# Second feed-forward in chunks beside the attention, one batch behind it

## The reference

```
x = x + attn_a(norm(x))                      # conv, pooled attention, gelu
x = x + ffn(norm(x))                         # first feed-forward
x = x + attn_b(norm(x))
x = x + ffn(norm(x))                         # second feed-forward
ffn(x)    = sum over 8 experts of (silu(x @ wg) * (x @ wu)) @ wd
attn_b(x): scores = q @ k / sqrt(8) + alibi_bias   (-inf for later keys)
           softmax(scores) @ v, then @ w_out
```

## Time and profile before

| | us |
|---|---|
| median of three runs (1867.92 to 1869.69) | 1868.59 |
| profiled execution | 1865.06 |
| its span | 1863.3 |
| TensorE busy | 1688.7 (91%) |
| VectorE busy | 1238.6 (66%) |
| ScalarE busy | 1042.8 (56%) |
| GpSimd busy | 228.8 (12%) |

### The profile page before, as it was taken

How to read it: one execution, slowest core, us unless ns; L and a number is a source line. 1 busy time by engine, 2 the same in 40 slices (tenths; PEclk the granted TensorE clock), 3 DMA queues, 4 the chain that set the end, 5 groups by cost and what they waited for, 6 DMA issues and landing times.

```text
span 1863.3 us, 29609 instructions
## 1 busy us (share of the span) xinstructions
PE 1688.7 (91%) x10268; PEld 1150.8 (62%) x10268; DVE 1238.6 (66%) x2140; ACT 1042.8 (56%) x1695; POOL 228.8 (12%) x456
## 2 busy tenths in 40 slices
PE   4589999999999999958888888887899999999998
PEld 2257677767777877723333333332788888888887
DVE  3558566756676677667777777773566666666665
ACT  3435745565465556526666666666455555555554
POOL 4702000200120011111111111112000000000000
PEclk8699999999999999959999999999899999999999
DMA  5100000000000033240202112010000000000000
GB/s 169 38 1 1 1 1 1 0 0 1 0 0 0 1 101 102 79 113 25 58 25 58 42 30 58 24 26 2 0 1 7 6 0 5 6 6 0 7 6 7
DMA packets 60507, 46.83 MB, mean 25 GB/s; under 512 B 7647, under 2 KB 58222, under 8 KB 60398
## 3 DMA queue, kind: packets, MB, share of 16 engines
q1 hardware_dynamic: 60142, 45.30, 8.4%
q10 hardware_dynamic: 256, 0.10, 0.0%
HBM read 28.20 MB, written 17.17 MB: 24 GB/s over the span
## 4 chain that ended last, share of the span: by engine, by line
PE 79%; DVE 8%; ACT 7%; issue 4%; POOL 2%; DMA 0%; ACTq 0%; DVEq 0%; POOLq 0%
PE ps L783 12%; PE ps L784 12%; PE ps L782 12%; PE ps L789 6%; PE ps L790 6%; PE ps L791 6%; PE ps L896 6%; ACT pr L1187 4%; PE ps L641 4%; DVE negp L1482 4%; PE ps L880 3%; PE ps L855 3%; PE ps L710 2%; PE ps L664 2%; PE ps L717 1%
## 5 line engine op out<-in xcount | busy, mean ns | idle before, releaser
L1415 DVE TENSOR_TENSOR hid<-sg,ps 128x512 f32<-128x512 f32 x512 | 350.5, 685 | 388.6 <-PE ps L784 345.6
L1112 ACT ACTIVATE sg<-ps 128x512 f32<-128x512 f32 x512 | 306.1, 598 | 481.3 <-PE ps L784 477.4
L782 PE MATMUL ps<-xn_hi,w_hi 128*128 128x512 f32 x1024 | 426.0, 416 | 2.2 <-DVE xn_lo L1275 1.4
L784 PE MATMUL ps<-xn_hi,w_lo 128*128 128x512 f32 x1024 | 403.1, 394 | 0.0
L783 PE MATMUL ps<-xn_lo,w_hi 128*128 128x512 f32 x1024 | 402.9, 393 | 0.0
L1187 ACT ACTIVATE pr<-ps 128x1024 f32<-128x1024 f32 (+1 forms) x320 | 295.2, 942 | 161.0 <-PE ps L843 110.1
L1432 DVE TENSOR_TENSOR h_lo<-hid,h_hi 128x512 fp32r<-128x512 f32 x512 | 363.6, 710 | 1.4 <-ACT h_hi L1129 1.2
L1129 ACT CAST h_hi<-hid 128x512 fp32r<-128x512 f32 x512 | 313.9, 613 | 1.2 <-DVE hid L1415 0.9
L1482 DVE TENSOR_REDUCE negp<-ps 128x2 f32<-128x1024 f32 (+2 forms) x224 | 248.8, 1144 | 67.2 <-PE ps L843 36.6
L782 PEld LDWEIGHTS ps<-xn_hi,w_hi 128*128 128x128 f32 x1024 | 193.6, 189 | 55.1 <-issue 10.8
L783 PEld LDWEIGHTS ps<-xn_lo,w_hi 128*128 128x128 f32 x1024 | 193.3, 189 | 52.8 <-issue 11.5
(11 more groups left out here) (161 smaller groups left out, 1463.9 us busy)
## 6 DMA issues: line engine op xcount, KB each, us to landing
qs<-qd SPq DMA_DIRECT2D x64, 96.0 KB
ks<-kd SPq DMA_DIRECT2D x64, 96.0 KB
kd<-qkp SPq DMA_DIRECT2D x16, 256.0 KB, 2.9
qd<-qkp SPq DMA_DIRECT2D x8, 384.0 KB, 2.6
x<-in_hidden SPq DMA_DIRECT2D x4, 512.0 KB, 6.5
raw<-in_Wg SPq DMA_DIRECT2D x4, 512.0 KB, 4.5
raw<-in_Wu SPq DMA_DIRECT2D x4, 512.0 KB, 5.4
raw<-in_Wd SPq DMA_DIRECT2D x4, 512.0 KB, 6.7
```

What stands on the lines that cost most here:

```text
L782: pe.matmul(dst, w_hi[m][:, w], xn_hi[:, h, :], start=True, stop=False)
L784: pe.matmul(dst, w_lo[m][:, w], xn_hi[:, h, :], start=False, stop=True).then_inc(f[sig], 1)
L1112: a.activation(sg[:, c % 2, :], bank(c % 2), ACT.Silu).then_inc(f["silu"], 1)
L1415: v.tensor_tensor(hid[:, c % 4, :], sg[:, c % 2, :], bank(2 + c % 2), ALU.mult).then_inc(f["prod"], 1)
```

## The change

Units 0 to 4 stay as they are, but in unit 4 the first tile's norm, transpose and split for the second feed-forward are made. From unit 5 (`MIX`) on, each turn whose number does not leave 4 when divided by 5 carries one chunk of the second feed-forward, 16 a unit, 176 of the 256 in all; tiles go one batch behind the attention. The other 80 follow after unit 15 (`rest_of_ffn`), with the last batch's results and projection between them. In the mixed turns:

- Scores have one pair of banks (0, 1), jobs another (2, 3), which also takes all transposes; down has bank 4, gate 5, weighed values 6, up 7. A score waits for the exponential of the turn before, a job for the reduction of the turn before, gate for the first gated product of the chunk before, up for the second.
- Silu is replaced: ScalarE takes tanh(gate / 2), VectorE makes (tanh + 1) x gate and then x up, which is twice the product; the tile's result is halved in its copy. In the last 80 chunks silu stays, with a factor 2, and two banks each for gate and up.
- The rest `h_lo` is made by GpSimd, in the last 80 chunks by VectorE.
- Down stands two chunks behind gate and up. Each weigh step stands in the turn after its last exponential (`TURNS_TO`).
- `pr` has two buffers from unit 5 on and `vp` 9 columns a head where it had 32. The loops over pairs of tiles are gone: all is written out.

```diff
+MIX = 5
+CHUNKS = TILES * CH
+FFN_TURNS = [k for k in range(NG_S) if k % 5 != 4]
+BESIDE = (UNITS - MIX) * len(FFN_TURNS)
+S_BANK, J_BANK, Y_BANK, O_BANK = 0, 2, 4, 6
+def chunk_at(n, k):
+    if k < 0:
+        n, k = n - 1, k + NG_S
+    return (n - MIX) * len(FFN_TURNS) + FFN_TURNS.index(k) if n >= MIX and k in FFN_TURNS else None
+def values_at(n):
+    return VALUES_AT if n < MIX else TURNS_TO
+def gate_bank(q):
+    return 5 if q < BESIDE or q % 2 == 0 else 0
+def up_bank(q):
+    return 7 if q < BESIDE or q % 2 == 0 else 1
+Y_AT, STATS_AT, NORM_X_AT, XT_AT = (2, 4), 22, 24, 26
...
+def rest_of_chunk(q):
+    pool.wait_ge(FS[1]["hhi"], q + 1)
+    g.tensor_tensor(h_lo[:, q % 2, :], hid[:, q % 4, :], h_hi[:, q % 2, :].bitcast(F32),
+                    ALU.subtract).then_inc(FS[1]["hlo_pool"], 1)
+for n in range(MIX, UNITS):
+    for k, (st, _) in enumerate(TURNS):
+        if st in MASKED and TURNS_TO[st] == k + 1:
+            mask_step(n, st)
+        if chunk_at(n, k - 1) is not None:
+            rest_of_chunk(chunk_at(n, k - 1))
+        if k == 1:
+            split_max(n * 2 + 1)
+        if k == 9 and n % 2 == 0:
+            norm_of_tile((n - MIX + 1) // 2)
+        if k == 14 and n + 1 < UNITS:
+            split_max(n * 2 + 2)
+for t in range(BESIDE // CH + 1, TILES):
+    norm_of_tile(t)
...
+    def gate_up(q):
+        c, h = q % CH, q // CH % 2
+        w = slice(c * P, (c + 1) * P)
+        if c == 0:
+            pe.wait_ge(f["xlo"], q // CH + 1)
+        if q == 0:
+            pe.wait_ge(T["ctx"], MIX * 2 - 1)
+        if 0 < q <= BESIDE:
+            pe.wait_ge(f["half"], q)
+        if q == BESIDE + 1:
+            pe.wait_ge(T["exp"], UNITS * NG_S)
+        if q >= BESIDE + 2:
+            pe.wait_ge(f["prod"], q - 1)
+        for m, sig, dst in ((0, "gate", bank(gate_bank(q))), (1, "up", bank(up_bank(q)))):
+            if m == 1 and 0 < q <= BESIDE:
+                pe.wait_ge(f["prod"], q)
+            pe.matmul(dst, w_hi[m][:, w], xn_hi[:, h, :], start=True, stop=False)
+            pe.matmul(dst, w_hi[m][:, w], xn_lo[:, h, :], start=False, stop=False)
+            pe.matmul(dst, w_lo[m][:, w], xn_hi[:, h, :], start=False, stop=True).then_inc(f[sig], 1)
+    def down(q):
+        c, t = q % CH, q // CH
+        w, dst = slice(c * P, (c + 1) * P), bank(Y_BANK)
+        pe.wait_ge(f["hhi"], q + 1)
+        if q < BESIDE:
+            pe.wait_ge(f["hlo_pool"], q + 1)
+        else:
+            pe.wait_ge(f["hlo"], q - BESIDE + 1)
+        if c == 0 and t:
+            pe.wait_ge(f["y_out"], t)
+        pe.matmul(dst, w_hi[2][:, w], h_hi[:, q % 2, :], start=(c == 0), stop=False)
+        pe.matmul(dst, w_hi[2][:, w], h_lo[:, q % 2, :], start=False, stop=False)
+        pe.matmul(dst, w_lo[2][:, w], h_hi[:, q % 2, :], start=False, stop=(c == CH - 1)
+                  ).then_inc(f["dn"], 1)
+    def chunk(q):
+        gate_up(q)
+        if q >= 2:
+            down(q - 2)
+    def unit_beside_ffn(n):
+        b, g = divmod(n, NG)
+        more = n < UNITS - 1
+        begins = n % 2 and n > MIX
+        for k in range(NG_S):
+            for c in range(2):
+                if k == FIRST_OF_C[c]:
+                    pe.wait_ge(T[f"m_loaded{c}"], n * 32 + 32)
+            scores(n, k)
+            if k == 3:
+                pe.wait_ge(T["ctx"], n * 2)
+            if k == 4 and g == 0:
+                pe.wait_ge(T["c_out"], b * 2 - 1)
+            if k == 4 and begins:
+                pe.wait_ge(f["xadd"], (n - MIX) // 2)
+            if k == 5:
+                pe.wait_ge(T["m_out"], n * 2 + 2)
+            if k == 6 and g == 0:
+                pe.wait_ge(T["xadd"], b * 2 - 1)
+            if k == 8 and g == 0:
+                pe.wait_ge(T["c_out"], b * 2)
+            if k == 10 and g == 0:
+                pe.wait_ge(T["xadd"], b * 2)
+            if k == 13 and n % 2 == 0:
+                pe.wait_ge(f["xlo"], (n - MIX + 1) // 2 + 1)
+            if k == 16 and more:
+                pe.wait_ge(T["m_out"], n * 2 + 3)
+            if k == 18:
+                pe.wait_ge(T["ctx"], n * 2 + 1)
+            if more:
+                next_max(n, k)
+            if chunk_at(n, k) is not None:
+                chunk(chunk_at(n, k))
+            if more and k in (2, 3, 4, 5, 7, 9, 12, 15, 17):
+                pe.wait_ge(T["reduced"], (n + 1) * NG_S + k + 1)
+            if k == 2:
+                result_T(n - 1, 0, J_BANK)
+            if k == 3 and begins:
+                result_of_tile_T((n - MIX) // 2 - 1)
+            if k == 4:
+                maxima_T(n * 2 + 1, J_BANK)
+            if g == 0:
+                if k in (3, 7):
+                    context_T(b - 1, k // 4, J_BANK)
+                if k in (5, 9):
+                    project_out(b - 1, k // 6, J_BANK)
+            if k == 12 and n % 2 == 0:
+                input_T((n - MIX + 1) // 2, J_BANK)
+            if k == 15 and more:
+                maxima_T(n * 2 + 2, J_BANK)
+            if k == 17:
+                result_T(n, 1, J_BANK)
+            values(n, k)
+    def rest_of_ffn():
+        for q in range(BESIDE, CHUNKS):
+            c, t = q % CH, q // CH
+            chunk(q)
+            if q == BESIDE:
+                values(UNITS, 0)
+            if q == BESIDE + 3:
+                pe.wait_ge(T["ctx"], UNITS * 2 - 1)
+                result_T(UNITS - 1, 0, J_BANK)
+            if q in (BESIDE + 4, BESIDE + 6):
+                context_T(B - 1, (q - BESIDE - 4) // 2, J_BANK)
+            if q in (BESIDE + 5, BESIDE + 7):
+                project_out(B - 1, (q - BESIDE - 5) // 2, J_BANK)
+            if c == Y_AT[1]:
+                result_of_tile_T(t - 1)
+            if c == XT_AT and t + 1 < TILES:
+                if t == BESIDE // CH:
+                    pe.wait_ge(T["xadd"], B * 2)
+                else:
+                    pe.wait_ge(f["xadd"], t)
+                input_T(t + 1, J_BANK)
+        for q in (CHUNKS - 2, CHUNKS - 1):
+            down(q)
+        pe.wait_ge(f["xadd"], TILES - 1)
+        result_of_tile_T(TILES - 1)
...
+    def half_tanh(q):
+        act.wait_ge(f["gate"], q + 1)
+        a.activation(sg[:, q % 2, :], bank(gate_bank(q)), ACT.Tanh, scale=0.5).then_inc(f["silu"], 1)
+    def first_of_chunk(q):
+        act.wait_ge(f["prod"], q + 1)
+        a.copy(h_hi[:, q % 2, :], hid[:, q % 4, :]).then_inc(f["hhi"], 1)
+    def unit_beside_ffn(n):
+        b, g = divmod(n, NG)
+        more = n < UNITS - 1
+        for k in range(NG_S):
+            exponentials(n, k, ps[:, S_BANK:S_BANK + 2, :])
+            if k == 1:
+                result_out(n - 1, 0)
+            if k == 2 and n % 2 and n > MIX:
+                result_of_tile_out((n - MIX) // 2 - 1)
+            if k == 15:
+                result_out(n, 1)
+            if chunk_at(n, k - 1) is not None:
+                first_of_chunk(chunk_at(n, k - 1))
+            if chunk_at(n, k) is not None:
+                half_tanh(chunk_at(n, k))
+            if k == 4:
+                maxima_copy(n * 2 + 1, J_BANK)
+            if k == 6 and more:
+                place_values((n + 1) // NG, (n + 1) % NG)
+            if g == 0 and k in (3, 7):
+                context_out(b - 1, k // 4, J_BANK)
+            if k == 12 and n % 2 == 0:
+                input_out((n - MIX + 1) // 2, J_BANK)
+            if k == 15 and more:
+                maxima_copy(n * 2 + 2, J_BANK)
...
+    def gated(q):
+        dve.wait_ge(f["silu"], q + 1)
+        v.scalar_tensor_tensor(hid[:, q % 4, :], sg[:, q % 2, :], 1.0, bank(gate_bank(q)),
+                               ALU.add, ALU.mult).then_inc(f["half"], 1)
+        dve.wait_ge(f["half"], q + 1)
+        dve.wait_ge(f["up"], q + 1)
+        v.tensor_tensor(hid[:, q % 4, :], hid[:, q % 4, :], bank(up_bank(q)), ALU.mult).then_inc(f["prod"], 1)
+    def unit_beside_ffn(n):
+        b, g = divmod(n, NG)
+        for k in range(NG_S):
+            if n < UNITS - 1:
+                reduce_job(k, ps[:, J_BANK:J_BANK + 2, :], (n + 1) * NG_S)
+            if chunk_at(n, k) is not None:
+                gated(chunk_at(n, k))
+            if k == 2:
+                normalise(n - 1, 0, J_BANK)
+            if k == 3 and n % 2 and n > MIX:
+                add_tile((n - MIX) // 2 - 1)
+            if g == 0 and k in (5, 9):
+                add_projection(b - 1, k // 6, J_BANK)
+            if n % 2 == 0:
+                if k == 8:
+                    tile_stats((n - MIX + 1) // 2)
+                if k == 10:
+                    tile_norm((n - MIX + 1) // 2)
+                if k == 12:
+                    tile_rest((n - MIX + 1) // 2, J_BANK)
+            if k == 17:
+                normalise(n, 1, J_BANK)
```

More of the change, by code:

```diff
@@ L243, in build @@
         s = {n: sem(n) for n in names}
-        FF_NAMES = "st mv rs norm xT xhi xlo gate up silu prod hhi hlo dn y_done y_out yT xadd".split()
+        FF_NAMES = "st mv rs norm xT xhi xlo gate up silu half prod hhi hlo hlo_pool dn y_done y_out yT xadd".split()
```

(42 more changed lines are left out.)

345 lines of the change are left out of this document (207 added, 138 removed).

## The result

The changed kernel takes 1894.16 us (median of four runs, 1892.46 to 1895.25) against 1869.03 (1867.92 to 1869.69) on the same chip: ratio 1.0134, 95% interval 1.0117 to 1.0152. It is slower by 25.1 us where 22 were forecast. The profiled execution took 1895.25 us, its span 1893.4.

A forecast was written before the change was run, and what follows sets the result against it. TensorE was 91% busy: the second feed-forward pure TensorE, units 5 to 14 waiting in turns. Span 979.4 + 3 + 665.6 + 57 + 180 = 1885, 22 us longer; from the 1868.6 median 1890 us, range 1846 to 1932.

The forecast's parts named there:

- Start and end: Up to unit 5's start 979.4 us plus 3 for the first tile's preparation; last 80 chunks and close 180 us.
- The mixed part: Units 5 to 15 with their chunks: 655 + 10.6 + 57 = 723 us, where 701 would be even.
- Tile changes: Between half-array scores or jobs and whole-array chunks: 0.12 in, 0.15 out, 0.27 us a chunk, 4.3 a unit; bounds 0 to 0.40.
- rival 1: Weight loads overlap long products, changes cost 0.10 a chunk, holes 4.5 us: unit 60.7, time 1837 us, faster; chance 0.28.
- Holes: TensorE's waits in mixed units, mainly turns 4 and 9, where VectorE runs behind: 6.6 us a unit on average.
- clock 1.00 from unit 5 on: Sign to look for: TensorE's granted clock stays at its full level from unit 5 on.
- What was compared: Average unit 29.7 us and its 16 chunks 33.1 take 62.9 apart; mixed, a unit was put at 65.5.
- Rival 2: In chunk turns exponential, copy, tanh and two products run 0.5 late, gate waits every turn: 70 us more, 1960; chance 0.08.
- The slack of 0.15 to 0.2: In chunk turns VectorE's gated products finish 0.2 and 0.15 us before TensorE wants the next gate and up.
- Rival 3: Exponential and tanh reload ScalarE's tables, two loads of 1.28 a chunk turn: 264 us more, near 2150; chance 0.03.
- GpSimd and the loads at nothing: In mixed units GpSimd's subtraction (1.28 us x 16) is hidden and doesn't slow VectorE; data loads and instruction fetches cost nothing.
- the same subtraction is taken off VectorE: In mixed units the subtraction goes to GpSimd, relieving VectorE, put at 48 us busy of some 65 a unit.

The follow-up runs named there:

- `maxima_at5`: Changed kernel, units opening no batch: maxima's product and copy moved from turn 4 behind turn 5's chunk, needless reduction waits removed; 1879.15 us, ratio to before 1.0059.
- MIX series: Changed kernel with chunks beside attention only from unit 9, 13 or 15, not 5: 1882.09, 1866.32, 1859.69 us; ratios to before 1.0071, 0.9998, 0.9959.
- `weigh_inside`: Changed kernel with the weigh step between gate/up and down in chunk turns, one more change of tile each: 1917.02 us, ratio to before 1.0270.

## Why the prediction was right

The mechanism held: the price of tile changes and the holes outweigh what the mixing hides. That 22 came so near to 25 is partly luck, for two sizes were off in opposite directions.

- **Start and end.** Unit 5's first score started at 982.36, 3.0 later than before, as put. The 80 chunks left and the close: 180 us forecast, 180 measured.
- **The mixed part.** From 982.36 to 1713.0 it is 730.6 us, forecast 723 (655 + 10.6 + 57), break-even 701. This is the whole error of 8 us in the span; between the medians of one chip it is 25 against 22. Units 5 to 14 take 670.5 where 665.6 was forecast, unit 15 takes 60.2 where 57 was.
- **Tile changes.** 0.27 a chunk taken, 0.28 read, 0.20 to 0.26 by experiment for an added pair. The choice inside the bounds 0 to 0.40 decided the sign: at rival 1's 0.10 the 176 chunks would take 176 x 0.18 = 32 us less, more than the whole loss. The way in was placed before the first gate product; it shows half there, half between it and the next.
- **Holes.** In units 7, 9, 11 and 13 about 0.70 and 1.32 in turn 4 and 1.33 in turn 9, where 0.8, 1.4 and 1.4 stood. In the even units (and unit 5) 1.32 to 1.60 in turn 4 where 1.4 stood, and in turn 9 of units 6, 10 and 14 1.82 where 2.6 did. Right in place, and `maxima_at5` shows that they lie on the path. But the sum was too large: TensorE's idle times in units 5 to 14 are 55.8 us, 5.6 a unit with those of the batch openers, where 6.6 without them was forecast.
- **The term that was missing** is the clock, "clock 1.00 from unit 5 on": it falls 10.2 us short of that in units 5 to 14 (an estimate from the windows above), 1.0 a unit. It would more than cover the 7.6 us missing; the holes forecast too large hid most of it, and what is left over, 0.5 to 0.8 us a unit by estimate, is TensorE's own work above the forecast.
- **What was compared.** 62.9 us for a unit and its chunks apart counts chunks at 2.07. The second feed-forward before took 546.8 / 256 = 2.14 a chunk with its tile work. And unit 15's first score before starts at 1274.86, so that the ten units ahead of it took 29.5 each. 29.5 + 34.2 = 63.7 is the fair figure, and 67.0 - 63.7 = 3.3 (670.5 us for ten units) is the 3.3 a unit of the MIX series.
- **Rival 2** (the gated chain): VectorE waits for the tanh 143 times, yet over all gate and up products (L1020) TensorE idles 5.3 us, 4.5 of it for `hid`, of which 1.9 in one wait of unit 5. The slack of 0.15 to 0.2 held. **Rival 3**: no load beside a tanh.
- **GpSimd and the loads at nothing:** the rest on GpSimd was hidden, VectorE's products stayed at 0.687 beside it. But "the same subtraction is taken off VectorE" was worth 5 us at most by the medians.

## What to carry to other kernels

Before two stages are woven into one stream, work out TensorE's own time of the weave with about 0.2 to 0.3 us for each pass between tile shapes and back; if that already lies near the time of the two apart, what is left are the holes, and the weave has to give up buffers, which makes new ones. Weave where the engine runs with holes and at a slow clock (unit 15 here), not where a ring of banks already keeps it busy. Put a waiting product behind long work of the same engine, not in the turn that has none, and let a wait stand only where something uses the bank it guards.

## Not expected of the hardware

- The granted clock fell to 0.52 for 3.6 us behind two holes of 0.70 and 1.32 us, in a stretch where TensorE is busy over 90%. Behind lone holes of 1.32 to 1.60 it stayed at 1.00. In the run without chunks, whose turns hold waits of 1.06 to 1.33 again and again, it was 0.77 to 0.81 on average over 495 us.
- A change of tile costs on both sides: 0.10 to leave the whole array for a half, 0.08 before and 0.10 behind the first product of the whole array. A weigh step (nine columns a head) between whole-array products costs about the same, 0.09 before it and 0.11 behind the next product (`weigh_inside`).
- Two table loads a turn made ScalarE the bound at 4.75 us a turn, with no gap at all, and TensorE's mean clock fell to 0.936 for the span (0.967 with tanh).
